# Layer-3 attention: the penalties of both sequences made on VectorE in four fused pieces, GpSimd left with the weighing

## The chip, the cores and the metric

The kernel runs on one core of a Trainium2 chip. The metric is the device time of one execution in microseconds (us), the median over several runs. A core has five engines that run on their own and meet through semaphores: TensorE (PE, with its weight loads as PEld), VectorE (DVE), ScalarE (ACT), GpSimd (POOL) and SyncE (SP).

## What is computed

The reference is a network of four layers over 16 sequences of 256 tokens with 128 features; each layer is an attention-like part whose output is gated by the SiLU of a feed-forward part. The change touches only the attention of layer 3, which weights each probability by a penalty made from a learned gate per token:

```python
g = jax.nn.sigmoid(hidden_states @ Wg + bg)          # one gate per token
Z_I, Z_J = g, jnp.swapaxes(g, 1, 2)
res = (1.0 - Z_I) * jnp.maximum(1.0 - Z_I - Z_J, 0.0) + Z_I * jnp.minimum(1.0 - Z_I + Z_J, 1.0)
scope = jnp.clip(jnp.power(s - 2, 1.0 - g) + 2.0 - abs_ij, 1e-32, 1.0)
log_pen = jnp.log(jnp.maximum(res * scope, 1e-32))
probs = jax.nn.softmax(q @ k.T / np.sqrt(8) + log_pen, axis=-1)     # 16 heads of 8
ctx = probs @ v
```

The kernel adds no logarithm: it multiplies exp(scores) by the penalty. Penalties of a sequence are 256x256 numbers, the same for all heads, held as two tiles of 128x256.

## The kernel before

The 16 sequences are worked in eight passes of two sequences (NB = 2). Layers 0 and 1 run per pass, layer 2 over all, then a loop of eight passes does `layer3_attention` and `layer3_ffn`. Each is a block in which the five engines run written-out programs, tied by semaphores.

Within `layer3_attention` the attention is cut into eight batches, `BATCHES = NA * NB * 2`. `batch(n)` gives (a, sq, i) = (n // 4, n // 2 % 2, n % 2): batches 0, 1, 4, 5 belong to sequence 0, batches 2, 3, 6, 7 to sequence 1. A batch has NR = 4 units, u = 4n to 4n + 3, each a tile `PT[:, u % 12]` of 128x512 (keys by queries of one head). What happens to batch n:

- PE `scores(n)` (L253): 16 matmuls, waits for the maxima of batch n - 1. `scores` are written in PE's order before the rest of batch n - 1.
- VectorE `take_max(n)` (L407): two reductions over them. PE `turn_max(n)` (L262) turns them, VectorE `add_max(n)` (L418) makes from them and the queries QM, which holds the subtracted maximum.
- PE `scores_turned(n, pair)` (L280): the scores again, transposed, two units a time; ScalarE `exps` (L369) makes PT of each.
- The weighing of PT by the penalties PEN: unit 3 of each batch by VectorE (`weigh`, L426), units 0 to 2 by GpSimd (L1562). Batch 0 alone was weighed wholly by VectorE.
- PE `values(j)` (L294) after both batches 2j and 2j + 1 are weighed. In PE's order it stands between the two pairs of batch 2j + 2.

PT has 12 units, so the exponentials of batch 3 wait for `values(0)`. The PE order is: scores(0); then for each n: turn_max(n), scores(n + 1), scores_turned(n, 0), for even n from 2 values(n/2 - 1), scores_turned(n, 1); at the end the last values, totals and output (copied to S at L1546).

The penalties of a sequence were eleven operations in `penalties(eng, sq, link)` (L1442 to L1457): VectorE made those of sequence 0 right after `take_max(1)`, GpSimd those of sequence 1 from the moment that AJ = 1 - GJ and NI = -GI (L1537, L1538) were there. Only then, and after VectorE's own, could GpSimd begin to weigh batch 1. `link` makes the engine wait for its own last instruction.

Of the kernel before, what the change touches and what calls it, by code (L numbers as in the profile page):

```python
# [8 lines left out]
ALU = mybir.AluOpType  # L9
# [4 lines left out]
SEQ = 256  # L14
# [4 lines left out]
NA, NR = 2, 4  # L19
# [92 lines left out]
LN_SEMS = "ln_centred ln_square ln_var ln_rstd xn_ready "  # L112
GATE_SEMS = "gate_log gate_arg gate_sigmoid "
LINKS = "act_link dve_link pool_link "
# [98 lines left out]
BATCHES = NA * NB * 2  # L213
STBANKS = 3
PSLOTS = 3 * NR
# [3 lines left out]
def batch(n):  # L219
    return n // (2 * NB), n // 2 % NB, n % 2  # L220
# [18 lines left out]
def att_tensor(nc, pe, s, c, w, b, PB, w_out, masked, beside=None):  # L239
    VT, MXP = c.VT, c.MXP  # L240

    def scores(n):
        a, sq, i = batch(n)
        if n == 0:
            pe.wait_ge(s.q_copied, 1)
            pe.wait_ge(s.k0_copied, 2)
        if n:
            pe.wait_ge(s.max_taken, 2 * n)
        for qt in range(2):
            q0 = sq * SEQ + qt * 128  # L250
            for r in range(NR):
                rows = slice(32 * r, 32 * r + 32)
                last = nc.tensor.matmul(PB[:, r, qt * SEQ:(qt + 1) * SEQ], b.QP[rows, a, q0:q0 + 128],  # L253
                                        b.KP[rows, a, i, sq * SEQ:(sq + 1) * SEQ], start=True, stop=True)
        last.then_inc(s.scores_ready, 1)

    def turn_max(n):
        pe.wait_ge(s.max_taken, 2 * n + 2)
        if n >= 3:
            pe.wait_ge(s.ctx_copied, (n - 1) // 2)  # L260
        for qt in range(2):
            last = nc.tensor.transpose(PB[:, 7, SEQ + qt * 128:SEQ + qt * 128 + 128], MXP[:, n % 2, qt, :], c.ident)  # L262
        last.then_inc(s.turned, 1)

    def scores_turned(n, pair):
        a, sq, i = batch(n)
        first = NR * n + 2 * pair
        if pair == 0:
            pe.wait_ge(s.qm_ready, n + 1)
        if n == 0 and pair == 0:  # L270
            pe.wait_ge(s.v_copied, 1)
            pe.wait_ge(s.q_copied, 2)
            pe.wait_ge(s.k1_copied, 2)
        if first >= 2:
            pe.wait_ge(s.exp_done, first - 1)
        for kt in range(2):
            k0 = sq * SEQ + kt * 128
            for u in (first, first + 1):
                rows = slice(32 * (u % NR), 32 * (u % NR) + 32)
                last = nc.tensor.matmul(PB[:, 4 + u % STBANKS, kt * SEQ:(kt + 1) * SEQ], b.KP[rows, a, i, k0:k0 + 128],  # L280
                                        b.QM[rows, n % 2, :], start=True, stop=True)
        last.then_inc(s.st_ready, 2)

    def values(j):
        a, sq = divmod(j, NB)
        if masked:
            pe.wait_ge(s.weighed_dve, NR + 2 * j + 1)
            pe.wait_ge(s.weighed_pool, (NR - 1) * (2 * j + 1))
        else:
            pe.wait_ge(s.exp_done, 2 * NR * (j + 1))  # L290
        for i in range(2):
            for kt in range(2):
                for r in range(NR):
                    last = nc.tensor.matmul(PB[32 * r:32 * r + 32, 7, 0:SEQ], VT[:, 2 * sq + kt, 8 * a + 2 * r + i, :],  # L294
                                            b.PT[:, (NR * (2 * j + i) + r) % PSLOTS, kt, :], start=i == 0 and kt == 0,
                                            stop=i == 1 and kt == 1, tile_position=(0, 32 * r))
        last.then_inc(s.ctx_ready, 1)

    def totals(a):
        pe.wait_ge(s.ctx_copied, 2 * (a + 1))  # L300
        nc.tensor.matmul(PB[:, a, :], c.sumsel, b.OS[:, a, :], start=True, stop=True).then_inc(s.den_ready, 1)

    scores(0)
    for n in range(BATCHES):
        turn_max(n)
        if n + 1 < BATCHES:
            scores(n + 1)
        else:
            totals(0)
            if beside:  # L310
                beside(0)
        scores_turned(n, 0)
        if n and n % 2 == 0:
            values(n // 2 - 1)
        scores_turned(n, 1)
    values(BATCHES // 2 - 1)
    if beside:
        beside(1)
    totals(1)
    if beside:  # L320
        beside(2)
    for a in range(NA):
        pe.wait_ge(s.z_ready, a + 1)
        if a == 0:
            pe.wait_ge(s.exp_done, NR * BATCHES)
        last = nc.tensor.matmul(PB[:, 4, :], w_out[:, a * 128:(a + 1) * 128], b.Z[:, a, :], start=a == 0, stop=a == NA - 1)
    last.then_inc(s.att_ready, 1)
# [73 lines left out]
def att_vector(nc, dve, s, c, b, PB, link, masked, before=None, beside=None):  # L401
# [17 lines left out]
                                ALU.add).then_inc(s.qm_ready, 1)  # L419

    def weigh(n):
        for r in range(NR) if n == 0 else (NR - 1,):
            u = NR * n + r
            dve.wait_ge(s.exp_done, u + 1)
            pt = b.PT[:, u % PSLOTS]
            nc.vector.tensor_tensor(pt, pt, b.PEN[:, 2 * batch(n)[1]:2 * batch(n)[1] + 2, :], ALU.mult).then_inc(s.weighed_dve, 1)  # L426

    take_max(0)
    if before:
        before(0)  # L430
    for n in range(BATCHES):
        add_max(n)
        if masked and n >= 2:
            weigh(n - 1)
        if n + 1 < BATCHES:
            take_max(n + 1)
        if masked and n == 0:
            before(1)
            weigh(0)
    if masked:  # L440
        weigh(BATCHES - 1)
    if beside:
# [988 lines left out]

L3_SEMS = LN_SEMS + ATT_SEMS + GATE_SEMS + LINKS + "y_mixed yT_ready y_taken x_gated next_loaded gate_ready gate_raw gate_exp gate_u gi_ready gi_negated pen_dve pen_pool "


def layer3_attention(nc, c, w, r, it, x_mid, s_mid, PB):
    with ExitStack() as ctx:
        s = semaphores(nc, ctx, L3_SEMS)
        b = att_buffers(nc, ctx, "l3", PEN=[TT, SEQ], T1=[TT, SEQ], T2=[TT, SEQ], GA=[T + TT], GU=[T + TT], GJ=[T], AJ=[T],  # L1440
                        PJ=[T], GI=[TT], NI=[TT], YM=[2, TT, 128])

        def penalties(eng, sq, link):

            both, gates = slice(2 * sq, 2 * sq + 2), slice(sq * SEQ, (sq + 1) * SEQ)
            two = lambda x: x[:, gates].unsqueeze(1).broadcast_to([128, 2, SEQ])
            for t in (2 * sq, 2 * sq + 1):
                eng.tensor_scalar(b.T2[:, t, :], b.AJ[:, gates], b.GI[:, t:t + 1], 1.0, ALU.add, ALU.min)  # L1448
                last = eng.tensor_scalar(b.T1[:, t, :], b.AJ[:, gates], b.NI[:, t:t + 1], 0.0, ALU.add, ALU.max)
            link(last)  # L1450
            eng.tensor_tensor(b.T1[:, both], b.T1[:, both], two(b.AJ), ALU.mult)
            link(eng.tensor_tensor(b.T2[:, both], b.T2[:, both], two(b.GJ), ALU.mult))
            eng.tensor_tensor(b.T1[:, both], b.T1[:, both], b.T2[:, both], ALU.add)
            link(eng.tensor_tensor(b.PEN[:, both], c.dist.rearrange("p (t q) -> p t q", q=SEQ), two(b.PJ), ALU.add))
            link(eng.tensor_scalar(b.PEN[:, both], b.PEN[:, both], 1e-32, 1.0, ALU.max, ALU.min))
            link(eng.tensor_tensor(b.PEN[:, both], b.PEN[:, both], b.T1[:, both], ALU.mult))
            return eng.tensor_scalar(b.PEN[:, both], b.PEN[:, both], 1e-32, None, ALU.max)  # L1457

        with nc.Block() as block:
            @block.sync  # L1460
# [49 lines left out]
            def _(dve):  # L1510
                link = Link(dve, s.dve_link)
# [20 lines left out]
                                               op1=ALU.subtract).then_inc(s.gate_u, 1)  # L1532

                def penalty(part):
                    if part == 0:
                        dve.wait_ge(s.gi_ready, 2)
                        nc.vector.tensor_scalar(b.NI[:], b.GI[:], -1.0, None, ALU.mult)  # L1537
                        nc.vector.tensor_scalar(b.AJ[:], b.GJ[:], -1.0, 1.0, ALU.mult, ALU.add).then_inc(s.gi_negated, 1)  # L1538
                        dve.wait_ge(s.gi_negated, 1)
                    else:  # L1540
                        penalties(nc.vector, 0, link).then_inc(s.pen_dve, 1)
                        dve.wait_ge(s.pen_dve, 1)

                att_vector(nc, dve, s, c, b, PB, link, True, penalty)
                dve.wait_ge(s.att_ready, 1)
# [1 line left out]

            @block.gpsimd
            def _(pool):
                link = Link(pool, s.pool_link)  # L1550
                pool.wait_ge(s.gi_negated, 1)
                pool.wait_ge(s.gi_ready, 2)
                penalties(nc.gpsimd, 1, link).then_inc(s.pen_pool, 1)
                pool.wait_ge(s.pen_pool, 1)
                pool.wait_ge(s.pen_dve, 1)
                for n in range(1, BATCHES):
                    sq = batch(n)[1]
                    for r in range(NR - 1):
                        u = NR * n + r
                        pool.wait_ge(s.exp_done, u + 1)  # L1560
                        pt = b.PT[:, u % PSLOTS]
                        nc.gpsimd.tensor_tensor(pt, pt, b.PEN[:, 2 * sq:2 * sq + 2, :], ALU.mult).then_inc(s.weighed_pool, 1)  # L1562
# [562 lines left out]
```

## Time and profile before

| | before |
|---|---|
| median of 3 runs | 4293.75 us (4279.51 to 4311.54) |
| the profiled execution | 4289.45 us |
| its span (first to last instruction) | 4287.8 us |
| busy: PE / DVE / ACT / POOL | 3135.6 / 2390.9 / 1757.2 / 1207.0 us |
| mean granted TensorE clock | 0.811 of 2.4 GHz |

Times in the trace are from the span's start. A timeline row gives start, duration, engine, line, operation, output <- input, and the count of instructions that were merged into it; brackets hold the engine's idle time before and who ended it. Line numbers with an L are those of the kernel.

### The profile page before, as it was taken

To read this page: it belongs to the slowest core of one execution; us is meant where nothing else is said; L and a number is where in the kernel's file an instruction comes from. 1 tells how busy PE (TensorE), PEld (TensorE's weight loads), DVE (VectorE), ACT (ScalarE), POOL (GpSimd) and SP (SyncE) were. 2 spreads that over 40 slices of the span, in tenths; PEclk is the share of its full clock that TensorE was granted. 3 is DMA by queue.
4 is the path that set the end of the run, shared out by engine and by line. 5 is a ranking of instruction groups with operands and counts; after the bars stand their busy time and mean duration, and the time that the engine had idled before them with its cause. 6 is when DMAs were issued, how large, how long until landed. Compare 5 with 4: busy or idle time off the path is not lost. (4 is left out here: it accounts for less than half of the span.)

```text
span 4287.8 us, 54316 instructions
## 1 busy us (share of the span) xinstructions
PE 3135.6 (73%) x20266; PEld 1705.2 (40%) x20266; DVE 2390.9 (56%) x3405; ACT 1757.2 (41%) x3556; POOL 1207.0 (28%) x878
## 2 busy tenths in 40 slices
PE   6888888888234888887677676776777768678687
PEld 3444444444121444433344343443434434334343
DVE  3444444344373777887665555565555655555555
ACT  2333333333223556655334344253443534435344
POOL 0000000000341445555353331442413424233242
PEclk9888888888556999998879788597886977868779
DMA  2000000000221333322200000000000000000001
GB/s 94 8 7 7 5 7 2 7 7 8 89 79 33 82 87 92 91 80 72 75 1 6 8 6 8 1 6 8 6 6 3 6 8 3 6 6 6 8 1 8
DMA packets 82171, 112.05 MB, mean 26 GB/s; under 512 B 9920, under 2 KB 47296, under 8 KB 81344
## 3 DMA queue, kind: packets, MB, share of 16 engines
q1 hardware_dynamic: 76608, 98.31, 7.7%
q0 software_dynamic: 5376, 11.02, 1.1%
q8 instruction: 145, 2.38, 0.2%
q14 instruction: 42, 0.34, 0.0%
HBM read 82.55 MB, written 26.74 MB: 25 GB/s over the span
## 5 line engine op out<-in xcount | busy, mean ns | idle before, releaser
L369 ACT ACTIVATE l_PT<-PB 128x512 f32<-128x512 f32 x512 | 277.9, 595 | 551.1 <-PE PB L280 551.1
L280 PE MATMUL PB<-l_QM,l_KP 32*128 32x256 f32 x2048 | 378.3, 500 | 131.9 <-DVE l_QM L418 76.1
L1411 POOL TENSOR_TENSOR l_ST<-l_ST,l_CT 128x1024 f32<-128x1024 f32 x128 | 316.4, 2472 | 354.6 <-DVE l_ST L1350 354.6
L407 DVE TENSOR_REDUCE keep_MXP<-PB 128x4 f32<-128x1024 f32 x256 | 301.5, 1220 | 108.2 <-PE PB L253 108.2
L1350 DVE TENSOR_TENSOR_SCAN l_ST<-l_DA,l_DB 128x1024 f32<-128x1024 f32 x128 | 357.5, 2793 | 4.4
L280 PEld LDWEIGHTS PB<-l_QM,l_KP 32*128 32x128 f32 x2048 | 243.9, 245 | 257.2 <-ACT l_PT L369 99.6
L1562 POOL TENSOR_TENSOR l_PT<-l_PT,l_PEN 128x512 f32<-128x512 f32 x168 | 212.9, 1287 | 206.0 <-ACT l_PT L369 206.0
L703 POOL MEMSET l_KV<- 128x4 f32 x8 | 0.8, 104 | 923.2 <-POOLq L109 923.2
L1344 DVE TENSOR_TENSOR l_DB<-PB,l_BT 128x1024 f32<-128x1024 f32 x128 | 155.2, 1213 | 136.2 <-PE PB L1110 136.2
L1273 ACT ACTIVATE l_DA<-PB,keep_aneg 128x510 f32<-128x510 f32 x256 | 161.0, 683 | 163.2 <-DVE l_ST L1350 88.6
L1731 ACT ACTIVATE l3f_PP<-PB,l3f_MN 128x128 f32<-128x128 f32 x512 | 144.2, 371 | 186.4 <-DVE l3f_MN L1787 186.4
L253 PE MATMUL PB<-l_KP,l_QP 32*128 32x256 f32 x2048 | 208.1, 537 | 12.3 <-issue 12.3
L1767 DVE SCALAR_TENSOR_TENSOR l3f_CS<-PB,w3fs,consts 128x512 f32<-128x512 f32 x256 | 175.6, 745 | 67.5 <-ACT l3f_SQ L1704 63.9
L294 PE MATMUL PB<-l_PT,keep_VT 128*32 128x256 f32 x2048 | 182.7, 518 | 34.7 <-POOL l_PT L1562 22.4
L1110 PE MATMUL PB<-l_DL,consts 32*128 32x512 f32 x512 | 165.3, 682 | 56.7 <-ACT l_DA L1273 42.5
L1838 POOL TENSOR_TENSOR l3f_PP<-l3f_PP,l3f_RS 128x512 f32<-128x512 f32 x128 | 133.0, 1039 | 231.7 <-DVE l3f_RS L1793 231.7
L418 DVE TENSOR_TENSOR l_QM<-l_QP,PB 128x256 f32<-128x256 f32 x128 | 53.8, 421 | 257.3 <-PE PB L262 254.3
L1833 POOL TENSOR_TENSOR l3f_CS<-l3f_CS 128x512 f32<-128x512 f32 x64 | 95.6, 1494 | 355.9 <-DVE l3f_CS L1767 355.9
L1601 PE MATMUL PB<-l3f_HS,w3fs 128*128 128x512 f32 x256 | 143.1, 688 | 36.9 <-DVE l3f_HS L1748 36.9
L1110 PE MATMUL PB<-l_DU,consts 32*128 32x512 f32 x512 | 158.6, 679 | 0.0
L1448 POOL TENSOR_SCALAR l_T<-l_AJ,l_GI 128x256 f32<-128x256 f32 x16 | 18.3, 1147 | 493.1 <-DVE l_AJ L1538 493.1
L1653 PE MATMUL PB<-consts,l3f_PP 128*128 128x128 f32 x512 | 89.0, 301 | 88.5 <-POOL l3f_PP L1838 88.5
(408 smaller groups left out, 6797.5 us busy)
## 6 DMA issues: line engine op xcount, KB each, us to landing
l_WB<-in_w2f_dram SPq DMA_DIRECT2D x80, 320.0 KB, 3.0
l_WB<-in_w2f_dram SPq DMA_DIRECT2D x80, 258.0 KB, 2.7
l_XR<-xs_mid SPq DMA_DIRECT2D x80, 64.0 KB, 1.8
ys_mid<-l_YO SPq DMA_DIRECT2D x80, 64.0 KB, 2.8
s_mid<-keep_S SPq DMA_DIRECT2D x17, 256.0 KB, 2.0
w3fs<-in_w3f_dram SPq DMA_DIRECT2D x1, 3127.0 KB, 18.2
keep_XI<-in_x_dram SPq DMA_DIRECT2D x9, 256.0 KB, 3.0
x_mid<-keep_X SPq DMA_DIRECT2D x9, 256.0 KB, 3.0
```

What stands on the lines that cost most here:

```text
L253: last = nc.tensor.matmul(PB[:, r, qt * SEQ:(qt + 1) * SEQ], b.QP[rows, a, q0:q0 + 128], b.KP[rows, a, i, sq * SEQ:(sq + 1) * SEQ], start= ...
L280: last = nc.tensor.matmul(PB[:, 4 + u % STBANKS, kt * SEQ:(kt + 1) * SEQ], b.KP[rows, a, i, k0:k0 + 128], b.QM[rows, n % 2, :], start=True ...
L294: last = nc.tensor.matmul(PB[32 * r:32 * r + 32, 7, 0:SEQ], VT[:, 2 * sq + kt, 8 * a + 2 * r + i, :], b.PT[:, (NR * (2 * j + i) + r) % PSL ...
L369: nc.scalar.activation(b.PT[:, u % PSLOTS].rearrange("p k q -> p (k q)"), PB[:, 4 + u % STBANKS, :], ACT.Exp).then_inc(s.exp_done, 1)
L407: nc.vector.tensor_reduce(dst[:, 2 * pair:2 * pair + 2, :, 16 + n % 2], PB[:, 2 * pair:2 * pair + 2, :].rearrange("p r (t k) -> p r t k", ...
L1110: return nc.tensor.matmul(PB[:, bank + e, :], c.rowsel[q:q + 32, i * 128:(i + 1) * 128], src[q:q + 32, k % 2, h, :], start=True, stop=True)
L1273: last = nc.scalar.activation(b.DA[:, g % 2, e, :].rearrange("p (s t) -> p s t", t=SEQ)[:, :, 1:SEQ], PB[:, e, :].rearrange("p (s t) -> p ...
L1344: nc.vector.tensor_tensor(b.DB[:, g % 2], PB[:, PAIR0:PAIR0 + 2, :], b.BT[:, k % 2, :].unsqueeze(1).broadcast_to([128, 2, T]), ALU.mult).t ...
L1350: nc.vector.tensor_tensor_scan(b.ST[:, g % RING].rearrange("p k t -> p (k t)"), b.DA[:, g % 2].rearrange("p k t -> p (k t)"), b.DB[:, g % ...
L1411: nc.gpsimd.tensor_tensor(b.ST[:, g % RING], b.ST[:, g % RING], b.CT[:, k % 2, :].unsqueeze(1).broadcast_to([128, 2, T]), ALU.mult).then_i ...
L1562: nc.gpsimd.tensor_tensor(pt, pt, b.PEN[:, 2 * sq:2 * sq + 2, :], ALU.mult).then_inc(s.weighed_pool, 1)
L1767: last = nc.vector.scalar_tensor_tensor(out=seq(b.CS[:, i % 2, 2 * half + j, :]), in0=seq(PB[:, 2 * (i % 2) + half, :]), scalar=scale, in1 ...
```

## The change

VectorE makes the penalties of both sequences, each in two pieces: `gate_products(sq)`, four fused operations of 128x256, and `penalties(sq, link)`, four operations with two inputs of 128x512 and a last clamp. `before(part)` is called with -1 (AJ and NI, as before), then 0, 1, 2, 3 behind `take_max(1)`, `take_max(2)`, `take_max(3)`, `take_max(4)`: products of sequence 0, penalties 0, products 1, penalties 1. The eleven operations a sequence become nine. VectorE weighs only unit 3 of every batch: unit 3 of batch 0 behind penalties 0, of batch 2 behind penalties 1, the others as before. GpSimd makes no penalties; it weighs units 0 to 2 of all eight batches (24 instead of 21), each behind `pen_ready` of its sequence. `values` waits for counts that fit.

```diff
@@ values(j)
-            pe.wait_ge(s.weighed_dve, NR + 2 * j + 1)
-            pe.wait_ge(s.weighed_pool, (NR - 1) * (2 * j + 1))
+            pe.wait_ge(s.weighed_dve, 2 * j + 2)
+            pe.wait_ge(s.weighed_pool, (NR - 1) * (2 * j + 2))
@@ att_vector
-        for r in range(NR) if n == 0 else (NR - 1,):
-            u = NR * n + r
-            dve.wait_ge(s.exp_done, u + 1)
-            pt = b.PT[:, u % PSLOTS]
-            nc.vector.tensor_tensor(pt, pt, b.PEN[:, 2 * batch(n)[1]:2 * batch(n)[1] + 2, :], ALU.mult).then_inc(s.weighed_dve, 1)
+        u = NR * n + NR - 1
+        dve.wait_ge(s.exp_done, u + 1)
+        pt = b.PT[:, u % PSLOTS]
+        nc.vector.tensor_tensor(pt, pt, b.PEN[:, 2 * batch(n)[1]:2 * batch(n)[1] + 2, :], ALU.mult).then_inc(s.weighed_dve, 1)
 
     take_max(0)
     if before:
-        before(0)
+        before(-1)
     for n in range(BATCHES):
         add_max(n)
-        if masked and n >= 2:
+        if masked and n >= 2 and n != 3:
             weigh(n - 1)
         if n + 1 < BATCHES:
             take_max(n + 1)
-        if masked and n == 0:
-            before(1)
-            weigh(0)
+        if masked and n < 4:
+            before(n)
+        if masked and n % 2 and n < 4:
+            weigh(n - 1)
@@ layer3_attention
+        def gate_products(sq):
+            both, gates, two = span(sq)
             for t in (2 * sq, 2 * sq + 1):
-                eng.tensor_scalar(b.T2[:, t, :], b.AJ[:, gates], b.GI[:, t:t + 1], 1.0, ALU.add, ALU.min)
-                last = eng.tensor_scalar(b.T1[:, t, :], b.AJ[:, gates], b.NI[:, t:t + 1], 0.0, ALU.add, ALU.max)
-            link(last)
-            eng.tensor_tensor(b.T1[:, both], b.T1[:, both], two(b.AJ), ALU.mult)
-            link(eng.tensor_tensor(b.T2[:, both], b.T2[:, both], two(b.GJ), ALU.mult))
-            eng.tensor_tensor(b.T1[:, both], b.T1[:, both], b.T2[:, both], ALU.add)
-            link(eng.tensor_tensor(b.PEN[:, both], c.dist.rearrange("p (t q) -> p t q", q=SEQ), two(b.PJ), ALU.add))
-            link(eng.tensor_scalar(b.PEN[:, both], b.PEN[:, both], 1e-32, 1.0, ALU.max, ALU.min))
-            link(eng.tensor_tensor(b.PEN[:, both], b.PEN[:, both], b.T1[:, both], ALU.mult))
-            return eng.tensor_scalar(b.PEN[:, both], b.PEN[:, both], 1e-32, None, ALU.max)
+                nc.vector.scalar_tensor_tensor(out=b.T2[:, t, :], in0=b.AJ[:, gates], scalar=b.GI[:, t:t + 1], in1=b.GJ[:, gates],
+                                               op0=ALU.add, op1=ALU.mult)
+                last = nc.vector.scalar_tensor_tensor(out=b.T1[:, t, :], in0=b.AJ[:, gates], scalar=b.NI[:, t:t + 1], in1=b.AJ[:, gates],
+                                                      op0=ALU.add, op1=ALU.mult)
+            return last
+
+        def penalties(sq, link):
+
+            both, gates, two = span(sq)
+            nc.vector.tensor_tensor(b.PEN[:, both], c.dist.rearrange("p (t q) -> p t q", q=SEQ), two(b.PJ), ALU.add)
+            link(nc.vector.tensor_tensor(b.T2[:, both], b.T2[:, both], two(b.GJ), ALU.min))
+            link(nc.vector.scalar_tensor_tensor(out=b.T1[:, both], in0=b.T1[:, both], scalar=0.0, in1=b.T2[:, both], op0=ALU.max, op1=ALU.add))
+            link(nc.vector.scalar_tensor_tensor(out=b.PEN[:, both], in0=b.PEN[:, both], scalar=1.0, in1=b.T1[:, both], op0=ALU.min, op1=ALU.mult))
+            return nc.vector.tensor_scalar(b.PEN[:, both], b.PEN[:, both], 1e-32, None, ALU.max)
@@ penalty(part), VectorE
+                    elif part % 2 == 0:
+                        gate_products(part // 2).then_inc(s.pen_products, 1)
                     else:
-                        penalties(nc.vector, 0, link).then_inc(s.pen_dve, 1)
-                        dve.wait_ge(s.pen_dve, 1)
+                        dve.wait_ge(s.pen_products, part // 2 + 1)
+                        penalties(part // 2, link).then_inc(s.pen_ready, 1)
+                        dve.wait_ge(s.pen_ready, part // 2 + 1)
@@ GpSimd
-                link = Link(pool, s.pool_link)
-                pool.wait_ge(s.gi_negated, 1)
-                pool.wait_ge(s.gi_ready, 2)
-                penalties(nc.gpsimd, 1, link).then_inc(s.pen_pool, 1)
-                pool.wait_ge(s.pen_pool, 1)
-                pool.wait_ge(s.pen_dve, 1)
-                for n in range(1, BATCHES):
+                for n in range(BATCHES):
                     sq = batch(n)[1]
+                    pool.wait_ge(s.pen_ready, sq + 1)
```

## Rows read from the trace of the kernel before

**Rows 1.** The page's first line.

```profile
span 4287.8 us, 54316 instructions
```

**Rows 2.** Windows, one per pass, AJ to end: busy (instructions) per engine, granted clock.

```profile
2147.93:2222.77 74.84, 53.36 (x392) 29.77 (x392) 47.48 (x54) 21.24 (x40) 41.59 (x32) 0.68 0.00 1
2412.81:2491.64 78.83, 57.65 (x392) 31.81 (x392) 47.64 (x54) 21.25 (x40) 41.61 (x32) 0.65 0.00 1
2683.73:2772.49 88.76, 68.93 (x392) 37.84 (x392) 48.02 (x54) 21.25 (x40) 41.22 (x32) 0.54 0.00 1
2961.89:3041.98 80.09, 59.02 (x392) 32.09 (x392) 47.49 (x54) 21.25 (x40) 41.57 (x32) 0.63 0.00 1
3232.98:3314.99 82.01, 61.69 (x392) 34.28 (x392) 47.36 (x54) 21.25 (x40) 41.61 (x32) 0.60 0.00 1
...
sum 643.74, PE 477.43 PEld 264.14 DVE 380.26 ACT 169.96 POOL 332.40; mean PE 59.68 PEld 33.02 DVE 47.53 ACT 21.24 POOL 41.55
```

**Rows 3.** Timeline of the first pass, from AJ (T) to the first values.

```profile
2147.93 0.42 DVE L1538 TENSOR_SCALAR l_AJ<-l_GJ 128x512 f32<-128x512 f32 x1
...
2150.77 2.36 DVE L407 TENSOR_REDUCE keep_MXP<-PB 128x4 f32<-128x1024 f32 x2 [1.57 <-PE PB L253]
...
2155.72 2.09 PE L253 MATMUL PB<-l_KP,l_QP 32*128 32x256 f32 x16
...
2164.43 2.50 DVE L426 TENSOR_TENSOR l_PT<-l_PT,l_PEN 128x512 f32<-128x512 f32 x4
2166.85 0.41 DVE L418 TENSOR_TENSOR l_QM<-l_QP,PB 128x256 f32<-128x256 f32 x1
...
2167.32 2.07 PE L280 MATMUL PB<-l_QM,l_KP 32*128 32x256 f32 x8 [9.51 <-DVE l_QM L418]
...
2176.43 3.64 PE L294 MATMUL PB<-l_PT,keep_VT 128*32 128x256 f32 x32
```

**Rows 4.** VectorE's groups: count | busy us, mean ns; L1457 of the first pass.

```profile
L155 DVE SCALAR_TENSOR_TENSOR keep_lnt<-keep_lnt,keep_lnr 128x256 f32<-128x256 f32 x96 | 40.8, 425 | 3.3
...
L163 DVE SCALAR_TENSOR_TENSOR l_DT<-l_DT,l_RG 128x512 f32<-128x512 f32 x32 | 22.1, 692 | 1.1
...
L1457 DVE TENSOR_SCALAR l_PEN<-l_PEN 128x512 f32<-128x512 f32 x1 | 0.4, 426 | 0.0
```

**Rows 5.** Timeline of the first pass: GpSimd's runs of three, VectorE beside the second.

```profile
2184.78 3.72 POOL L1562 TENSOR_TENSOR l_PT<-l_PT,l_PEN 128x512 f32<-128x512 f32 x3 [1.03 <-ACT l_PT L369]
...
2205.43 4.17 POOL L1562 TENSOR_TENSOR l_PT<-l_PT,l_PEN 128x512 f32<-128x512 f32 x3 [1.03 <-ACT l_PT L369]
...
2207.71 0.77 DVE L426 TENSOR_TENSOR l_PT<-l_PT,l_PEN 128x512 f32<-128x512 f32 x1 [2.75 <-ACT l_PT L369]
```

**Rows 6.** Timeline of the third pass (T = 2683.73): first values to second values.

```profile
2712.22 3.64 PE L294 MATMUL PB<-l_PT,keep_VT 128*32 128x256 f32 x32
...
2718.42 2.09 PE L253 MATMUL PB<-l_KP,l_QP 32*128 32x256 f32 x16
...
2720.58 2.36 DVE L407 TENSOR_REDUCE keep_MXP<-PB 128x4 f32<-128x1024 f32 x2 [0.17 <-PE PB L253]
...
2725.53 2.09 PE L253 MATMUL PB<-l_KP,l_QP 32*128 32x256 f32 x16
...
2729.24 3.64 PE L294 MATMUL PB<-l_PT,keep_VT 128*32 128x256 f32 x32
```

**Rows 7.** Timeline of the second pass (T = 2412.81): the same stretch.

```profile
2441.05 3.44 PE L294 MATMUL PB<-l_PT,keep_VT 128*32 128x256 f32 x32
...
2445.85 1.15 PE L253 MATMUL PB<-l_KP,l_QP 32*128 32x256 f32 x16
...
2454.34 3.62 PE L294 MATMUL PB<-l_PT,keep_VT 128*32 128x256 f32 x32
```

## What I expect of the change

> **What bounds the kernel now.** I read the page first: the span is 4287.8 us, the execution's own time 4289.45 us, 4.3 us under the median of 4293.75 us [rows 1]. The changed stage runs eight times, between 2148 us and 4127 us. The windows from each pass's AJ instruction (I call its start T, the only fixed point that both kernels share) to the end of the stage's last copy hold 643.74 us in all, 80.5 us a pass [rows 2]. So the whole change plays in 15% of the span; 1% of the time, about what a measurement of this kernel can tell from no change, is 43 us or 5.4 us a pass. PE's granted clock in those windows is 0.54 to 0.68, that is, the engine goes back and forth between 1.2 and 2.4 GHz, and the pass at 0.54 is 14 us longer than that at 0.68: the clock alone moves a pass by more than I am arguing about.
>
> Then the timeline of the first pass [rows 3]. VectorE ends the second maximum at T + 5.2, then makes the penalties of sequence 0 until 2164.43 (T + 16.5), weighs four tiles and only at T + 18.9 gives PE the next query (before L280 PE sat idle 9.51 us). The first `values` starts at T + 28.50. The reader is to see that this gap of some 10 us lies on the path: PE waits for VectorE. From there on PE sets the pace: in the third pass, at 1.2 GHz, one `values` follows the other after 17.02 us [rows 6]; in the second pass, with the clock rising under way, after 13.29 us [rows 7].
>
> **The part that goes.** VectorE's penalties between maxima 1 and QM(1) vanish there, with GpSimd's own penalties and three of the four tiles that VectorE weighed in batch 0. The first quarter, `gate_products(0)`, is four fused operations of 128x256; such a one takes 0.425 us [rows 4], so some 1.7 us from T + 5.1 to T + 6.8. PE turns the maxima only up to T + 7.8, where scores(2) starts [rows 3]: hidden, and QM(1) comes at T + 7.9 instead of T + 18.9. If that cover were gone it would cost those 1.7 us a pass.
>
> **Where the wait goes: first burst.** `values(0)` now needs all six of GpSimd's weighings of batches 0 and 1, and GpSimd may start only when penalties(0) are there. Scores(2) start at T + 7.8; a maximum starts 2.16 us after its scores and takes 2.36 us [rows 6], so maxima 2 end at T + 12.3. Penalties(0) are four two-input operations of 128x512 at 0.692 us and one tensor_scalar at 0.426 us [rows 4]: 3.2 us, T + 15.5. GpSimd weighs three tiles in 3.72 us [rows 5]: six take 7.45 us, plus 0.1 us to start. VectorE meanwhile does two weighings and `gate_products(1)`. A VectorE weighing in a run of three stretched the run to 4.17 us, 0.45 us more, and itself took 0.77 us [rows 5]. Two of them: 0.9 us. For the products no row shows one beside GpSimd: between nothing and 0.45 us each; I take half of 0.45, their size being half, for the two that fall into the burst: 0.5 us. Sum: 15.5 + 0.1 + 7.45 + 0.9 + 0.5 = T + 24.4. Against 28.50 the change gains 4.1 us here, not 10: PE, whose scores follow one another after 7.1 us in a batch without `values` [rows 6], has scores(3) and the turned scores behind them done by about T + 18.7 and then waits for GpSimd.
>
> **Second burst, which I think decides.** Batch 2 is weighed by GpSimd only after penalties(1), which stand behind maxima 4, and those behind `values(0)` in PE's order. In the cold template [rows 6] scores(4) start 6.20 us after `values(0)`, the maximum 8.36 us after it and ends at 10.72; with the clock risen [rows 7] scores(4) start at 4.80 and take 1.15, so maxima 4 end at about 8.4 (weigh(2) no longer stands before them). Then 3.2 us penalties(1), 0.1 us, 7.45 us for batches 2 and 3, and 0.9 us for weigh(2) and weigh(3) between: 11.65 us. So `values(1)` comes 22.4 us (at 1.2 GHz) or 20.0 us (risen) after `values(0)`, where it was 17.02 or 13.29 us. Two to one for the risen clock, 20.9: T + 45.3. Before, it was at T + 45.5 in the third pass [rows 6], T + 41.5 in the second [rows 7]. The gain of 4.1 us is more than spent.
>
> **The rest of the pass.** GpSimd has caught up; nothing after `values(1)` changes but its clock. PE has waited for some 5 us ahead of it, so it begins at 1.2 GHz, as in the second pass (`values` of 3.62 us there), whose rest took 2491.64 - 2454.34 = 37.3 us [rows 2, 7]; in the pass that never rose it took 2772.49 - 2729.24 = 43.25 us [rows 2, 6]. I weigh them three to one (of the eight passes one was as long as that, the three not shown had 239.2 us together [rows 2]; but here PE stalls twice): 38.8 us. A pass then lasts 45.3 + 38.8 = 84.1 us against 80.5: +3.6 us, eight times +29, and 4287.8 + 29 = 4317 for the span, 4323 on the median. The edits left (two semaphores renamed, `weigh(2)` put behind penalties(1), GpSimd 24 weighings for 21) cost nothing by themselves: QM(4) goes out at about V + 14.6 (V is the start of `values(0)`) where PE's scores(5), started at V + 13.3 [rows 6], still run until V + 15.4, and the three additional weighings are in the burst above.
>
> **The contention weighed.** The row shows a stretch of 0.45 us for a VectorE operation of 0.69 us alone. The Trainium skill, SBUF — State Buffer, section "Who interferes with whom", says that a VectorE instruction with two SBUF inputs and a GpSimd instruction that reads SBUF lock each other out, and the lock is held for the whole instruction. By that rule each weighing would cost GpSimd 0.69 us and each product 0.42 us, 1.35 us a pass more, 11 us in all, about 4334. It speaks against this change, which moves two-input VectorE work into GpSimd's bursts.
>
> **Bounds.** Low: no contention in either burst and the risen clock: 23.05 + 8.4 + 3.2 + 7.55 = T + 42.2, rest 37.3, 79.5 us: -1 us a pass, 4286. High: cold throughout, and each VectorE operation costing GpSimd its full length (0.69 and 0.42): 25.3 + 22.9 = 48.2, rest 43.25, 91.4 us: +11 us a pass, 4381.
>
> **Rivals.**
> 1. *The clock stays low.* The stalls before both `values` keep PE at 1.2 GHz in most passes: 24.4 + 22.4 + 43.25 = 90.1 us, +9.6, eight times +77: 4371. For it: two stalls a pass instead of one, and the pass that never rose [rows 2]. Against: only one of eight did that. 0.20.
> 2. *Second burst hidden (the faster side).* If PE's own work between the first two `values` covers penalties(1) and GpSimd's six weighings, only the 4.1 us of the first burst remain: -33 us, 4261. It decides where PE's 13.3 to 17.0 us exceed the chain's 20.0; the chain would have to lose 3 us or more, so weighings well below 1.24 us or maxima 4 taken earlier. 0.12.
> 3. *Gain and loss cancel.* Little contention and a quick clock, the low bound above: 4286 to 4300. 0.20.
> 4. *Forecast*, 4300 to 4350, 4323 the likeliest: 0.48.
>
> **Range and chances.** 4282 to 4368 leaves out most of rival 2 and the upper half of rival 1, some 2 in 10. Faster by over 1% (under 4251) needs rival 2 and a better clock besides: 0.05. Slower by over 1% (over 4337) takes nearly all of rival 1 and a third of the forecast's own: 0.35. Within 1%: 0.60.
>
> **What would show it.** Right: PE's long idle moves from before QM(1) to before the first two `values`, released by GpSimd L1562; GpSimd has two runs of six weighings, each beginning right after VectorE's penalties; `values(0)` near T + 24.4 and `values(1)` near T + 45; GpSimd's mean weighing near 1.3 us. Wrong: `values(1)` at T + 41 or less (the chain is shorter than I make it), `values` that wait for VectorE instead of GpSimd, or a granted clock in the passes far from 0.6, which would outweigh the rest.

## The result, and the profile after

| | before | changed |
|---|---|---|
| median of 20 runs each | 4283.09 us | 4302.61 us |
| ratio, 95% interval | | 1.0049 (1.0026 to 1.0072) |
| span of the profiled execution | 4287.8 us | 4288.9 us |
| eight passes, AJ to end of stage | 643.74 us | 658.81 us |

The changed kernel is half a per cent slower, 19.5 us between the two medians and 21 us by the ratio, which is within 1%. The two profiled executions differ by only 1.1 us, and that is chance: the layers ahead of the changed stage, which are the same code, took 28.7 us less in the changed kernel's execution (its first AJ instruction starts at 2119.28 us, before at 2147.93 us). So the totals of two profiles say nothing here. The passes show where the time goes, but their sum, too, is that of one execution and can be off by as much as the change is worth (e10, below, shows 30 us of it that the median doesn't have); how much a kernel gains is read from the ratios.

The windows of the changed kernel, first and fourth pass and the sum, answer to [rows 2]: window, length, then busy time and instructions of PE, PEld, DVE, ACT, POOL, the granted clock, and DMA.

```profile
2119.28:2203.74 84.46, 62.25 (x392) 34.66 (x392) 46.02 (x58) 21.25 (x40) 32.59 (x24) 0.60 0.00 1
...
2949.36:3030.37 81.01, 55.27 (x392) 30.88 (x392) 46.00 (x58) 21.25 (x40) 32.58 (x24) 0.67 0.00 1
...
sum 658.81, PE 456.91 PEld 253.58 DVE 368.06 ACT 169.99 POOL 260.71; mean PE 57.11 PEld 31.70 DVE 46.01 ACT 21.25 POOL 32.59
```

Three engines are busy for less time than before: GpSimd 261 us instead of 332, VectorE 368 instead of 380, PE 457 instead of 477; ScalarE is where it was (170). The stage is longer all the same, by 15 us. That is a question of waits. The list of who waited for whom, line, engine waited for, total, times and longest, of the changed kernel:

```profile
PE PB L294 <- POOL l_PT L1566: 122.4, 24, 6.3
```

and of the kernel before:

```profile
PEld PB L280 <- DVE l_QM L418: 87.2, 15, 10.3
PE PB L280 <- DVE l_QM L418: 76.1, 8, 9.6
```

PE's eight waits of 9.5 us for VectorE's query are gone from the list, and 122 us of waits for GpSimd's weighings stand in their place. The timeline of the changed kernel's first pass (T = 2119.28) shows where, and answers to [rows 3]:

```profile
2127.18 0.42 DVE L418 TENSOR_TENSOR l_QM<-l_QP,PB 128x256 f32<-128x256 f32 x1 [1.12 <-PE PB L262]
...
2131.51 0.68 DVE L1459 TENSOR_TENSOR l_PEN<-consts,l_PJ 128x512 f32<-128x512 f32 x1
...
2134.27 0.43 DVE L1463 TENSOR_SCALAR l_PEN<-l_PEN 128x512 f32<-128x512 f32 x1
2134.74 0.69 DVE L425 TENSOR_TENSOR l_PT<-l_PT,l_PEN 128x512 f32<-128x512 f32 x1
2134.78 8.90 POOL L1566 TENSOR_TENSOR l_PT<-l_PT,l_PEN 128x512 f32<-128x512 f32 x6 [46.77 <-ACT l_PT L369]
...
2139.68 1.48 DVE L1452 SCALAR_TENSOR_TENSOR l_T<-l_AJ,l_NI 128x256 f32<-128x256 f32 x1
...
2143.83 3.64 PE L294 MATMUL PB<-l_PT,keep_VT 128*32 128x256 f32 x32 [5.87 <-POOL l_PT L1566]
...
2152.19 2.36 DVE L407 TENSOR_REDUCE keep_MXP<-PB 128x4 f32<-128x1024 f32 x2 [1.63 <-PE PB L253]
...
2157.23 0.43 DVE L1463 TENSOR_SCALAR l_PEN<-l_PEN 128x512 f32<-128x512 f32 x1
...
2157.74 10.78 POOL L1566 TENSOR_TENSOR l_PT<-l_PT,l_PEN 128x512 f32<-128x512 f32 x8 [14.05 <-ACT l_PT L369]
...
2166.20 3.61 PE L294 MATMUL PB<-l_PT,keep_VT 128*32 128x256 f32 x32 [5.28 <-POOL l_PT L1566]
```

The query QM(1) goes out at T + 7.90, eleven us earlier than before. The penalties take 3.19 us and end at T + 15.4. GpSimd then weighs six tiles in 8.90 us, PE waits 5.87 us and starts `values(0)` at T + 24.55. The second burst starts only at T + 38.5, behind maxima 4 and penalties(1) (in the other passes at T + 36.4 to T + 36.9); PE waits another 5.28 us. In this pass `values(1)` is at T + 46.9, in the others at T + 44.9 to T + 45.3.

### The profile page after: what moved, and what is told of

It reads as the page before. It is cut to its first block and busy times, and to the rows that moved or that the text cites. A ratio compares the mean times of both kernels' runs of the same rounds, so it can differ in the third digit from the quotient of the medians.

```text
span 4288.9 us, 54324 instructions
## 1 busy us (share of the span) xinstructions
PE 3093.8 (72%) x20266; PEld 1684.5 (39%) x20266; DVE 2377.4 (55%) x3437; ACT 1757.4 (41%) x3556; POOL 1135.7 (26%) x814
## 5 line engine op out<-in xcount | busy, mean ns | idle before, releaser
L1566 POOL TENSOR_TENSOR l_PT<-l_PT,l_PEN 128x512 f32<-128x512 f32 x192 | 260.7, 1385 | 793.3 <-ACT l_PT L369 707.4
L280 PE MATMUL PB<-l_QM,l_KP 32*128 32x256 f32 x2048 | 356.1, 475 | 73.3 <-ACT l_PT L369 55.7
L280 PEld LDWEIGHTS PB<-l_QM,l_KP 32*128 32x128 f32 x2048 | 231.8, 234 | 192.2 <-ACT l_PT L369 97.0
L294 PE MATMUL PB<-l_PT,keep_VT 128*32 128x256 f32 x2048 | 181.1, 514 | 132.6 <-POOL l_PT L1566 122.4
L253 PE MATMUL PB<-l_KP,l_QP 32*128 32x256 f32 x2048 | 189.2, 495 | 15.6 <-issue 15.6
L294 PEld LDWEIGHTS PB<-l_PT,keep_VT 128*32 128x32 f32 x2048 | 79.9, 140 | 219.0 <-issue 188.3
L1605 PE MATMUL PB<-l3f_HS,w3fs 128*128 128x512 f32 x256 | 136.3, 659 | 36.9 <-DVE l3f_HS L1752 36.9
```

## The experiments

Each is a short edit; where only the order of calls on VectorE changes, the diff shows that order. The table gives means over the eight passes of each profiled execution, in us after the pass's AJ instruction: the start of the first and second `values`, the end of the stage, and what lies between the second `values` and the end. The last column is the ratio to the kernel before with its interval; the kernel before was run again beside each set. The sets (e1 to e4, e5 to e8, e9 and e10) were measured on three chips, so two kernels of different sets are compared by their ratios and not by their times.

| kernel | values(0) | values(1) | end | rest | ratio |
|---|---|---|---|---|---|
| before | 28.43 | 43.02 | 80.47 | 37.45 | 1 |
| changed | 24.55 | 45.37 | 82.35 | 36.98 | 1.0049 (1.0026 to 1.0072) |
| e1 penalties(1) earlier | 24.47 | 39.16 | 74.92 | 35.77 | 0.9913 (0.9876 to 0.9950) |
| e2 batch 0 on VectorE | 23.55 | 43.95 | 81.48 | 37.53 | 1.0097 (1.0063 to 1.0131) |
| e3 whole, early | 19.56 | 33.68 | 71.63 | 37.95 | 0.9877 (0.9830 to 0.9925) |
| e4 products together | 23.77 | 44.05 | 81.08 | 37.02 | one execution, 1.004 |
| e5 fusion alone | 27.70 | 40.43 | 76.05 | 35.62 | 0.9946 (0.9926 to 0.9965) |
| e6 e3 not fused | 20.13 | 35.27 | 71.62 | 36.36 | 0.9885 (0.9859 to 0.9912) |
| e7 PE fed in the waits | 24.56 | 43.49 | 77.98 | 34.49 | 0.9968 (0.9945 to 0.9991) |
| e8 e3, products in a gap | 18.62 | 32.74 | 71.00 | 38.26 | 0.9812 (0.9792 to 0.9832) |
| e9 e8, PE fed | 18.32 | 34.62 | 67.93 | 33.31 | 0.9813 (0.9771 to 0.9854) |
| e10 before, PE fed | 28.41 | 41.38 | 76.74 | 35.37 | 0.9994 (0.9966 to 1.0021) |

### e1: does the second burst's start set values(1)?

```diff
 take_max(3)
 gate_products(1)
+penalties(1)
 ...
 take_max(4)
-penalties(1)
```

> The changed kernel with one edit: penalties(1) stand behind take_max(3), right behind gate_products(1), and no longer behind take_max(4). T is the start of the AJ instruction of a pass. Theory (GpSimd's second burst is late because penalties(1) wait for maxima 4, and those for values(0)): values(0) stays at about T + 24.5; penalties(1) are ready by about T + 29; GpSimd weighs batch 2 at once, so values(1) follows values(0) after 13.3 to 17.0 us, at T + 38 to T + 41.5, not at T + 45.4; PE's idle time ahead of L294 by GpSimd, 122 us in the changed kernel, falls to about half; the kernel is 30 to 45 us faster than the changed one, some 4265 us. Rival (the GpSimd's rate, not its start, sets values(1)): values(1) stays within 1 us of T + 45.

In e1's second pass (T = 2428.58), timeline:

```profile
2453.13 3.64 PE L294 MATMUL PB<-l_PT,keep_VT 128*32 128x256 f32 x32 [5.86 <-POOL l_PT L1569]
...
2456.09 0.43 DVE L1464 TENSOR_SCALAR l_PEN<-l_PEN 128x512 f32<-128x512 f32 x1
2456.59 3.71 POOL L1569 TENSOR_TENSOR l_PT<-l_PT,l_PEN 128x512 f32<-128x512 f32 x3 [3.60 <-DVE l_PEN L1464]
...
2465.93 1.93 PE L294 MATMUL PB<-l_PT,keep_VT 128*32 128x256 f32 x32 [1.42 <-POOL l_PT L1569]
```

`values(0)` did not move, penalties(1) were ready at T + 27.9, and `values(1)` came at T + 36.8 to T + 41.6, on average 6.2 us earlier. The wait of the second `values` shrank from 5.28 to 1.42 us here; PE's waits for GpSimd fell from 122.4 to 81.9 us, a third rather than half. The kernel, one edit away from the changed one, is 0.9% faster than before, where the changed one is 0.5% slower: by the ratios 58 us between them (39 to 77 with both intervals), and 59 us by the passes of the two profiles, more than the 30 to 45 expected. The rival (GpSimd's rate sets `values(1)`) falls. What made the change a loss is where penalties(1) stand.

### e2 and e4: what sets values(0)

e2 gives VectorE all of batch 0 to weigh again (`values` then waits for the counts of the kernel before):

```diff
-        u = NR * n + NR - 1
-        dve.wait_ge(s.exp_done, u + 1)
+        for r in range(NR) if n == 0 else (NR - 1,):
+            u = NR * n + r
+            dve.wait_ge(s.exp_done, u + 1)
@@ GpSimd
-                for n in range(BATCHES):
+                for n in range(1, BATCHES):
```

> The changed kernel with the weighing of batch 0 wholly on VectorE again, GpSimd from batch 1 on. Theory (the six GpSimd weighings in a row set values(0)): GpSimd has three left, VectorE four of batch 0 that meet them, each side waiting for the other: VectorE done with batch 0 at about T + 20.5, values(0) at T + 22.5 to T + 23.5 instead of T + 24.55, values(1) 1 to 2 us earlier too, the kernel 8 to 15 us faster than the changed one. Rival (VectorE is the scarcer engine here and moving weighings to it costs as much as it frees): values(0) at T + 24.5 or later, no gain.

e4 takes gate_products(1) out of the first burst:

```diff
 take_max(1)
 gate_products(0)
+gate_products(1)
 ...
 take_max(3)
-gate_products(1)
```

> The changed kernel with gate_products(1) moved beside gate_products(0), behind take_max(1), out of GpSimd's first burst; nothing else. Theory (three of the four products each make a GpSimd weighing about 0.2 us longer, the lock between the two engines): GpSimd's first six weighings take 8.3 to 8.4 us instead of 8.90, values(0) comes at T + 23.9 to T + 24.1, and VectorE's four products of sequence 1 take 0.48 us each and not 1.48. Rival (the products' effect is in the noise, GpSimd's six are slow for another reason): 8.9 us again.

Timeline of the first pass, the burst in e2 and then the same in e4:

```profile
2153.54 5.70 DVE L426 TENSOR_TENSOR l_PT<-l_PT,l_PEN 128x512 f32<-128x512 f32 x4
2153.59 5.11 POOL L1567 TENSOR_TENSOR l_PT<-l_PT,l_PEN 128x512 f32<-128x512 f32 x3 [46.79 <-ACT l_PT L369]
```

```profile
2156.50 8.32 POOL L1569 TENSOR_TENSOR l_PT<-l_PT,l_PEN 128x512 f32<-128x512 f32 x6 [46.81 <-ACT l_PT L369]
```

e4 did what was expected of it: 8.32 us for the six weighings instead of 8.90, `values(0)` at T + 23.97 in that pass, and the products of sequence 1 took 0.48 us each. So the products cost GpSimd some 0.6 us, and the burst's length is indeed on the path. In e2 the two engines met on every tile: VectorE needed 5.70 us for four weighings, GpSimd 5.11 us for three. `values(0)` came one us earlier, at T + 23.55, just past the late end of what I had expected (22.5 to 23.5). The gain of 8 to 15 us for the kernel did not show: its ratio is 1.0097, rather above the changed kernel's 1.0049 than below it, though the passes of its profile are 0.9 us shorter. That GpSimd's six weighings hold `values(0)` is supported by the traces of both; that moving some to VectorE pays is not.

### e3 and e6: the pieces, and the fusion

```diff
 take_max(1)
 gate_products(0)
+penalties(0)
 ...
 take_max(2)
-penalties(0)
 ...
 take_max(3)
 gate_products(1)
+penalties(1)
 ...
 take_max(4)
-penalties(1)
```

> Products and penalties of a sequence in one piece again, but placed for GpSimd's start: sequence 0 whole behind take_max(1), sequence 1 whole behind take_max(3). Theory (what counts is when GpSimd may begin, and VectorE's fused 5 us are cheap enough to stand on PE's path): QM(1) goes out at about T + 10.4 instead of T + 7.9 (two us of PE idle), GpSimd starts at T + 10.1 instead of T + 15.5, values(0) at T + 21 to T + 22 bound by PE, values(1) at T + 35 to T + 39; a pass of 73 to 77 us against 82.4 in the changed kernel and 80.5 in the one before; 4225 to 4260 us, faster than both. Rival (splitting the penalties between maxima is what gains): the 2.5 us by which QM(1) is late push everything behind, values(0) stays at T + 24.5 or later and the kernel is no faster than the one with only penalties(1) moved.

e6 is e3 with the old eleven operations in place of the nine, cut into the same two functions (the four `tensor_scalar` in the first, seven operations in the second).

> The kernel with the penalties of sequence 0 whole behind take_max(1) and of sequence 1 whole behind take_max(3), all on VectorE, but made by the old eleven operations instead of the nine fused ones. Theory (fusing is worth only the operations it saves: four tensor_scalar of 0.2 to 0.25 us and three more two-input ones against four of 0.48): the eleven take 5.7 to 6.2 us where nothing runs on GpSimd, against 5.0; QM(1) 0.7 to 1.2 us later, values(0) at T + 20.5, values(1) 1 to 2 us later, the kernel 10 to 20 us slower than the fused one, still faster than before by 35 us or so. Rival (fusing is the main gain): 40 us or more lost against the fused one.

Timeline of e3's first pass (T = 2144.40), from the last of penalties(0) on:

```profile
2154.00 0.43 DVE L1464 TENSOR_SCALAR l_PEN<-l_PEN 128x512 f32<-128x512 f32 x1
2154.46 0.42 DVE L418 TENSOR_TENSOR l_QM<-l_QP,PB 128x256 f32<-128x256 f32 x1
2154.50 8.28 POOL L1569 TENSOR_TENSOR l_PT<-l_PT,l_PEN 128x512 f32<-128x512 f32 x6 [41.34 <-DVE l_PEN L1464]
...
2154.93 2.08 PE L280 MATMUL PB<-l_QM,l_KP 32*128 32x256 f32 x8 [0.65 <-DVE l_QM L418]
...
2164.05 3.64 PE L294 MATMUL PB<-l_PT,keep_VT 128*32 128x256 f32 x32
```

With penalties(0) in one piece QM(1) goes out at T + 10.1 instead of T + 7.9, and PE's wait for it is 0.65 us. GpSimd starts 5.4 us earlier, and `values(0)` at T + 19.65 waits for nobody. That was even earlier than expected (21 to 22); `values(1)` at T + 33.8 too, and the median of 4218 us lies below the 4225 to 4260 expected. The rival, that splitting the penalties between maxima is what gains, falls by the trace: splitting bought PE two us and cost GpSimd five, and `values(0)` comes 4.9 us earlier than in e1. For the whole kernel this is not shown: the intervals of e3 (0.9877) and e1 (0.9913) overlap.

The fusion is worth little. Unfused, VectorE needs 5.4 us for a sequence (T + 5.1 to T + 10.6) instead of 4.9, `values(0)` is 0.6 us later, and the kernels' intervals, 0.9877 (0.9830 to 0.9925) and 0.9885 (0.9859 to 0.9912), can't be told apart: 3 us between the ratios, give or take 23. The 10 to 20 us of loss that I had expected are not seen, nor are they excluded; the rival's 40 us or more are.

### e5: fusion alone in the kernel before

```diff
-                        penalties(nc.vector, 0, link).then_inc(s.pen_dve, 1)
+                        link(gate_products(0))
+                        fused(0, link).then_inc(s.pen_dve, 1)
```

The edit (`fused` is the changed kernel's `penalties(sq, link)`; GpSimd keeps the old function) leaves all else in place.

> The kernel before with only VectorE's penalties(0) made by the nine fused operations, in one piece at their old place behind take_max(1); GpSimd makes those of sequence 1 by the old eleven and weighs from batch 1 on, as before. VectorE's nine alone take 5.0 us. Theory (VectorE's 11.4 us in the kernel before were the lock with GpSimd's eleven, which run from T + 0.5 to T + 15 beside them, more than its own operations): every two-input operation still waits for a GpSimd one, the products 1.4 us each, the rest 1.0 to 1.7; the nine take 9 to 11 us, QM(1) goes out at T + 17 to T + 19 instead of T + 18.9, values(0) at T + 26.5 to T + 28.5, gain 0 to 15 us. Rival (fusing is what shortens VectorE's part): the nine take 5 to 6 us, QM(1) by T + 13.5, values(0) by T + 23, a gain of 40 us or more.

Timeline of e5's first pass, beginning and end of the nine:

```profile
2132.70 1.57 DVE L1466 SCALAR_TENSOR_TENSOR l_T<-l_AJ,l_GI,l_GJ 128x256 f32<-128x256 f32 x1
2132.72 1.27 POOL L1451 TENSOR_TENSOR l_T<-l_T,l_AJ 128x512 f32<-128x512 f32 x1
...
2140.86 1.63 DVE L1478 SCALAR_TENSOR_TENSOR l_PEN<-l_PEN,l_T 128x512 f32<-128x512 f32 x1
...
2142.53 0.72 DVE L1479 TENSOR_SCALAR l_PEN<-l_PEN 128x512 f32<-128x512 f32 x1
```

The nine take 10.6 us beside GpSimd's eleven, where they take 4.9 alone. So of the 11.4 us of VectorE before [rows 3] about half were waits for GpSimd within the instructions: the eleven take 5.4 us alone (e6). The kernel gained 0.54%, 23 us, more than the 0 to 15 expected, while `values(0)` moved only 0.7 us. That `values(1)` moved by 2.6 us is for the larger part the clock, which rose between the two `values` in all eight passes here (T + 40.0 to T + 40.9) and in five of the eight before (the other three, at a granted clock of 0.50 all along, have it at T + 45.5). Nothing of the edit asks for that. The traces don't show that the gain beyond the 0.7 us comes from the edit, or that it would be so again.

### e7 and e10: what the clock adds to a wait

```diff
@@ values(j), e7, in the changed kernel
         if masked:
+            for _ in range(22 if j < 2 else 0):
+                nc.tensor.matmul(PB[:, 7, 0:SEQ], c.identb, c.windowb[:, 0:SEQ], start=True, stop=True)
             pe.wait_ge(s.weighed_dve, 2 * j + 2)
@@ scores_turned(n, pair), e10, in the kernel before
+        if masked and n == 1 and pair == 0:
+            pe.wait_ge(s.exp_done, 3)
+            for _ in range(40):
+                nc.tensor.matmul(PB[:, 5, 0:SEQ], c.identb, c.windowb[:, 0:SEQ], start=True, stop=True)
         if pair == 0:
             pe.wait_ge(s.qm_ready, n + 1)
```

> The changed kernel with 22 idle matmuls of 128x256 ahead of values(0) and of values(1), into the part of the bank that values overwrites; they add work on PE and change no result. They fill the 5 us in which PE waits for GpSimd. Theory (the stalls also cost the clock: both values then start at 1.2 GHz, 3.64 us instead of 1.93, and what follows them too): values(0) stays at T + 24.5 but takes less than 3 us in most passes, values(1) at T + 43.5 to T + 44.5, the rest of a pass from values(1) on 34 to 35.5 us instead of 37.0, the kernel 15 to 30 us faster than the changed one. Rival (the clock's share is nothing: GpSimd's bursts set the pace whatever PE's clock): values(1) and the rest within 0.5 us of the changed kernel's, no gain.

> The kernel before with 40 idle matmuls of 128x256 in the 10 us in which PE waits for QM(1), into a bank that is free then; they change no result. It asks how much of the time between the kernels is the clock's alone. Theory (a wait on PE's path costs twice, its own length and the clock after it): values(0) moves from T + 28.4 to T + 25 to T + 26.5, because the scores and turned scores between run at 2.4 GHz, and the passes end 3 to 5 us earlier: 25 to 40 us faster than before, as much as the first wait taken away. Rival (the wait's length is what counts): values(0) within 0.5 us, the kernel within 10 us of before.

e7's first pass, timeline:

```profile
2148.25 4.73 PE L288 MATMUL PB<-windowb,identb 128*128 128x256 bf16 x22
...
2154.18 1.93 PE L296 MATMUL PB<-l_PT,keep_VT 128*32 128x256 f32 x32 [1.20 <-POOL l_PT L1568]
```

`values(0)` starts at T + 24.56 as in the changed kernel, but takes 1.93 us instead of 3.64 (in six of the eight passes; 3.3 and 3.4 in the other two): PE is at 2.4 and not at 1.2 GHz. `values(1)` comes at 43.5 instead of 45.4, the rest takes 34.5 instead of 37.0, and the kernel is 0.8% faster than the changed one by the ratios (0.9968 against 1.0049, the intervals apart), some 35 us where 15 to 30 were expected, with more work on PE. A pass ends 4.4 us earlier. So PE's clock was worth 4.4 us a pass on top of the two waits; the rival falls.

That the two waits take the clock away, as the expectation has it, is right only of the second. Ahead of `values(0)` PE was at 1.2 GHz before its wait began: the granted clock from AJ to `values(0)` is 0.50 in all eight passes of the changed kernel and 0.50 or 0.51 in all of the kernel before, and e3's first `values(0)`, which waits for nobody, takes 3.64 us too. There the idle matmuls raised the clock (22 of them took 4.73 us, 40 of the same in e10 4.68 us, so most of the 22 ran at half speed); the wait without them put the rise off. Ahead of `values(1)` the clock had risen in seven of the eight passes and was lost in the wait. The second pass of the changed kernel, PE's timeline:

```profile
2434.75 1.13 PE L280 MATMUL PB<-l_QM,l_KP 32*128 32x256 f32 x8 [2.53 <-DVE l_QM L418]
2442.19 3.64 PE L294 MATMUL PB<-l_PT,keep_VT 128*32 128x256 f32 x32 [6.30 <-POOL l_PT L1566]
```

e10 came out as its rival says, but does not decide between the two. Its 40 matmuls ran quicker than I had counted and were over 4.9 us before the query came; PE was back at 1.2 GHz (2.08 us for the eight that follow). From the timeline of one of its passes:

```profile
2463.49 4.68 PE L271 MATMUL PB<-windowb,identb 128*128 128x256 bf16 x40
2473.07 2.08 PE L284 MATMUL PB<-l_QM,l_KP 32*128 32x256 f32 x8 [4.90 <-DVE l_QM L422]
```

`values(0)` stayed at 28.41, and the kernel is as fast as before (0.9994). The passes of its one profile are 3.7 us shorter, 30 us for the eight, which its median does not bear out. What a fully bridged wait would have brought the kernel before stays open.

### e8 and e9: a version that beats both

```diff
@@ e8, after add_max(0), on top of e3
+        gate_products(0)
         take_max(1)
-        gate_products(0)
         penalties(0)
@@ e9, on top of e8, in values(j)
+            for _ in range({1: 10, 3: 14}.get(j, 0)):
+                nc.tensor.matmul(PB[:, 7, 0:SEQ], c.identb, c.windowb[:, 0:SEQ], start=True, stop=True)
```

> The kernel with whole penalties behind take_max(1) and take_max(3), with one step more: gate_products(0) moved ahead of take_max(1), where VectorE waits 1.57 us for PE. Theory (GpSimd's start sets what follows): penalties(0) are ready at T + 8.4 instead of T + 10.1, QM(1) at T + 8.4, values(0) at T + 18 to T + 18.7, bound by PE, values(1) about 1 us earlier too; 6 to 12 us faster than without that step, some 4208 us. Rival (values(1) is bound by penalties(1) and GpSimd, PE only waits longer there): values(0) earlier, values(1) where it was, no gain.

> The kernel with gate_products(0) ahead of take_max(1) and whole penalties behind take_max(1) and take_max(3), plus 10 idle matmuls of 128x256 ahead of values(1) and 14 ahead of the last values, where PE waits 2.5 and 2.6 to 3.3 us. They add PE work and change no result. Theory (the clock that PE loses in the waits is worth time only where PE sets the pace, which is the rest of the pass here): values(0) and values(1) stay at T + 18.6 and T + 32.7, values(1) takes less than 2.9 us in most passes, the rest of a pass 35 to 36.5 us instead of 38.3, the kernel 15 to 25 us faster than without them, some 4190 us. Rival (10 matmuls are too few to hold the clock and PE does the rest of the pass as before): within 5 us of the kernel without them.

VectorE waited 1.57 us ahead of take_max(1); the four products fit there. `values(0)` came at T + 18.6 in e8, where PE alone sets it, `values(1)` one us earlier than in e3, as expected. The gain on e3 is 0.65% by the ratios, 28 us (0.9812 at most 0.9832, 0.9877 at least 0.9830, so it may be far less); the passes of the profiles give 0.6 us each, 5 us, and 6 to 12 us had been expected. e8 is the fastest kernel by its ratio, 0.9812 (0.9792 to 0.9832): 1.9% faster than before, 2.4% faster than the changed one. In e9's profile the rest of a pass is shorter (33.3 instead of 38.3 us), but `values(1)` is later in five of the eight passes, at T + 37.9 in two. In these two PE never rose from 1.2 GHz between the two `values` (granted clock 0.50), and the ten idle matmuls, 2.31 us, stood on its path. The ratio is that of e8, and the expected gain of 15 to 25 us is not there.

## Why the prediction was right, point by point

It gave 4323 us (4282 to 4368) and within 1% as the likeliest; measured is 4302.61. The first median of the kernel before was 4293.75 us, that of 20 runs 4283.09. Against the first, from which the forecast was made, it was +0.7%; measured is +0.5% by the ratio. The mechanism came as forecast, waits moved from VectorE's query to GpSimd's two bursts; that the numbers came so close is in part luck, as the points below say.

- **The part that goes.** QM(1) expected at T + 7.9, is at T + 7.90. The products are hidden; they take 0.48 us each, not 0.425, which still fits. (Their scalar comes from memory, that of the row was a constant; whether that is the reason no run shows.)
- **First burst.** Penalties(0) 3.2 us, measured 3.19. The six weighings 7.45 + 0.9 + 0.5 = 8.85 us, measured 8.90. `values(0)` T + 24.4, measured 24.55. One by one, the six took 1.77, 1.70, 1.26, 1.48, 1.44 and 1.44 us: VectorE's two weighings cost GpSimd 0.51 and 0.45 us, and three products, not two, fell into the burst and cost 0.22, 0.18 and 0.18 us. That is the size of the row that I took the 0.45 from [rows 5]. The sum came out because a third product made up for a base that was 0.1 us too long. GpSimd's mean weighing over all 24 a pass is 1.39 us, where the sign of being right was near 1.3. The rule of the Trainium skill, SBUF — State Buffer, section "Who interferes with whom", was right that a VectorE instruction with two SBUF inputs and GpSimd block each other: three of VectorE's four products took 1.48 instead of 0.48 us. That GpSimd would be held for the whole instruction (0.69 and 0.48 us), as the prediction took from it, is not what these times show: GpSimd lost less than the instruction's record. (The section has the words on the whole instruction in its line on the two-port modes; of two SBUF inputs it says that they contend.)
- **Second burst.** `values(1)` 20.9 us after `values(0)`, at T + 45.3; measured 20.8 and T + 45.37. e1 shows that the chain is the one named: penalties(1) behind maxima 4 behind `values(0)`. The closeness is luck in part: the pass in which the clock stayed low took 22.4 us, just as the cold template said, but only one pass of eight was such, where one in three was forecast, and the other seven took 20.3 to 20.8 us, 0.3 to 0.8 more than the 20.0 said for them. The query QM(4) was said to cost nothing because PE's scores(5) would still run; in the second pass PE did wait 2.53 us for it, and that cost nothing because the wait for GpSimd came behind it.
- **The rest of the pass.** This was the term of the sum that was mis-sized: 38.8 us taken, 36.98 measured. PE did start `values(1)` at 1.2 GHz in all passes, as said; but no rest was longer than 38.6 us, none like the one of 43.25 us before, and I had given that case a quarter; and four passes, at 35.7 us, were below the 37.3 us of the quick case. With it the pass is 82.35 us instead of 84.1, +1.9 us instead of +3.6, and the eight passes +15 us instead of +29.
- **What I had at nothing.** The feed-forward part between two passes is the same code and took 192.6 us on average in the changed kernel's profile against 190.8 us before, +12 us over the seven. The experiments speak against the attention as its cause: the four profiles of e5 to e8, taken on one chip, all have 192.4 to 192.8 us, e5 among them, whose attention is nearly that of before; the six of the other two chips have 190.1 to 192.0 us, with 191.0 in e4, one moved call from the changed kernel. So these 12 us look like the chip's or the execution's; which, is open.
- **The rivals.** The second burst hidden: no, it is what costs. The clock low throughout: no. Gain and loss cancel: 4302.61 lies between its 4286 to 4300 and the middle of the forecast, at the low edge of the forecast's 4300 to 4350.

## What to carry to other kernels

When work moves off an engine whose wait is on the critical path, ask next which engine may then begin, and behind what; a producer that is cut into pieces to stay out of one engine's way can start its consumer later than it freed the first. Here 2 us more of VectorE on PE's path let GpSimd begin 5 us earlier (e3), and one call moved up by one maximum turned a loss of 0.5% into a gain of 0.9% (e1). The busy time, in the changed kernel lower for three engines and the same for the fourth, says nothing of that.

## What the runs showed of the hardware

- Two engines that both read two tiles from SBUF slow each other within the instructions, and a profile shows it as longer durations and not as idle time: nine VectorE operations took 4.9 us alone and 10.6 us beside GpSimd's; four weighings beside three of GpSimd 5.70 and 5.11 us, where alone they take 2.5 [rows 3] and 3.72 us [rows 5].
- PE can lose its clock in a wait of 6 us: in the changed kernel's second pass it works at 2.4 GHz, waits 6.30 us and does the 32 matmuls of `values` in 3.64 us. With idle matmuls in the first wait, the first `values` takes 1.93 us in six of eight passes (e7); a filling that ends 4.9 us early leaves nothing of that (e10). Slow matmuls behind a wait don't prove that the wait slowed them: e3's first `values(0)` takes 3.64 us with no wait ahead.
